# A mixture-of-experts FFN kernel on one core: its second transposes move from TensorE to VectorE squares and a trip through DRAM, the down product two blocks behind

## The chip, the cores and the metric

One core of a Trainium2 chip runs the whole kernel. The metric is the device time in microseconds (us), the median over runs of the program. Besides it there is one profiled execution, whose trace names every instruction, what it waited for, and every transfer.

## The reference

Two layers over x, [4, 512, 256] float32 (2048 tokens). The change touches the second only.

```
x = x + L0_xattn(layernorm(x), ctx_2048, lens)       # rms norms, a 256x256 projection, a decayed scan, a gather
z = layernorm(x)                                      # second layer
probs = softmax(z @ gate_w); top 2 of E = 8 experts, their weights scaled to sum 1
for i in range(8):
    h = silu(z @ w1[i]) * (z @ w3[i])                 # [tokens, 1024]; w1, w3: [256, 1024]
    out = out + (h @ w2[i]) * wi[..., None]           # w2: [1024, 256]; wi is 0 where expert i is not chosen
x = x + out
```

## The kernel before

The first layer, the router and the lists of tokens fill the first 108 us or so. Tokens are sorted by expert into blocks of 128 (at most 39 blocks; 37 here), and a block belongs to one expert. The FFN then runs one step per block, in order. `over_steps` (L288) unrolls step 0 and loops over pairs of steps; a word per step, from a table that VectorE makes, holds the block's expert, the expert of the block before and flags. The order of instructions in each engine's program is fixed by hand, in its own `step` function; semaphores join them.

Products are float32 made of three float32r products (`three`: hi by hi, hi by lo, lo by hi). So each operand exists as a rounded part and a rest: ScalarE copies (`split_hi` for weights, `xT`, `hT`), and VectorE subtracts (`split_lo`, `xT`, `hT`).

What TensorE does in step i, in this order (L1376):

- `up(slot, q, 0)`: half of the gate and up columns for block i, 12 multiplications of 512 columns
- `hT(i-1, 1)`: 4 transposes (with an identity) of the second half of block i-1's hidden rows into PSUM
- `xT(i+1)`: 2 transposes of the next block's input, gathered from DRAM
- `up(slot, q, 1)`: the other half, 12 multiplications
- `hT(i, 0)`: 4 transposes of the first half of block i
- `down(i-1)`: 24 multiplications of 256 columns for the block before, into one PSUM tile

ScalarE in step i: `silu` of half 0, the rounded copy of the transposes of block i-1's half 1, the same for `xT(i+1)`, `silu` of half 1, the copy of block i's half 0, then the weight splits of that step if its flags ask for one, and last `y(i-1)`, which scales the down product. VectorE: `h` (silu times the linear part) of half 0, the rest of `hT(i-1, 1)`, `meta`, the rest of `xT`, `next_index`, `h` of half 1, the rest of `hT(i, 0)`, then `split_lo` where ScalarE split.

The three parts of an expert's weights (w1, w3, w2; 1 MB each) are split into hi and lo during the first three steps of the expert before it, one part a step. SyncE loads them: experts 0 and 1 during the first layer, expert 2 just after step 0's splits, and expert e+3 when expert e+1's last part is split. GpSimd gathers the rows of block i+3 in step i (`block_rows`, L468) and adds the rows of block i-1 to the output in DRAM with an accumulating scatter (`add_rows`, L476). Each scatter waits until the one before has landed. After the last step `drain` does the last half block's transposes and the last down product.

Of the kernel before, what the change touches and what calls it, by code (L numbers as in the profile page):

```python
# [22 lines left out]
P = 128  # L23
B, S, D = 4, 512, 256
# [15 lines left out]
TABLE = 1 + 2 * STEP_PAIRS + 3  # L40

PREV_BIT = 3
F_CHUNK, F_W2, F_W3, F_LOAD, F_RUN = (1 << n for n in range(6, 11))
CHUNK_BIT = 11
OUT_INIT = 32
# [3 lines left out]
RAW_SEM = 48  # L49


def build(nc, x, ctx, lens, w_in, b_in, g_res, g_init, gate_w, w1, w3, w2, out):
# [12 lines left out]
    with stack:  # L65
# [6 lines left out]
        z_dram = nc.dram_tensor("z_rows", (T + P, D), f32, kind="Internal").ap()  # L72
        depool_dram = [nc.dram_tensor(f"depool_rows{b}", (S, D), f32, kind="Internal").ap() for b in range(B)]
# [103 lines left out]
        with ExitStack() as early:  # L177
# [9 lines left out]
        dg = sb("dg", [P, 2, TPB, D], f32)  # L187
# [59 lines left out]
            hT0hi_ready hT0lo_ready hT1hi_ready hT1lo_ready xT_done xThi_ready xTlo_ready  # L247
# [7 lines left out]
        blk_in = [sem(f"blk_in{q}") for q in range(2)]  # L255

# [6 lines left out]
        def raw_load(eng, e, slot, signal, parts=(0, 1, 2)):  # L263

            for m in parts:
                to = raw_dn[:, ds(slot, 1)] if m == 2 else raw_up[:, ds(slot, 1), m]
                eng.dma_start(to, (w1, w3, w2)[m][ds(e, 1)].rearrange("o (k p) n -> p (o k) n", p=P))\
                   .then_inc(signal, 16)

        def step_word(eng, i):  # L270
            entry, top = table[0:1, ds(i, 1)], (3 << CHUNK_BIT) - 1
# [7 lines left out]
        def chunk_of(word):  # L279
            return (word >> CHUNK_BIT).with_bounds(min_val=0, max_val=2)  # L280
# [8 lines left out]
        def over_steps(eng, body):  # L289

            body(0, 0, 0, step_word(eng, 0))
            with eng.Fori(0, STEP_PAIRS) as pair:
                word = step_word(eng, pair * 2 + 1)
                with eng.If(word & F_RUN):
                    body(pair * 2 + 1, 1, pair, word)
                    word = step_word(eng, pair * 2 + 2)
                    with eng.If(word & F_RUN):
                        body(pair * 2 + 2, 0, pair + 1, word)

        def block_count(eng):  # L300
            eng.wait_ge(s["blocks_ready"], 1)
            return eng.value_load(blocks_i[:, :], min_val=E, max_val=BLOCKS)

        def at_end(eng, blocks, drain):

            with eng.If(blocks & 1):
                drain(blocks - 1, 0)
            with eng.If((blocks + 1) & 1):
                drain(blocks - 1, 1)
# [17 lines left out]
        def _(sp):  # L327
# [31 lines left out]
            parts = [(e, m) for e in range(2) for m in range(3)]  # L359
            for k in range(B + 2):  # L360
# [17 lines left out]
                for e, m in parts[max(k - 1, 0):k] if k < B + 1 else parts[k - 1:]:  # L378
# [1039 lines left out]
```

## Time and the profile before

| | |
|---|---|
| median of 3 runs | 485.99 us (485.35 to 486.03) |
| the profiled execution | 486.02 us |
| its span, first to last instruction | 484.3 us |
| mean granted TensorE clock | 0.938 |
| busy: TensorE / VectorE / ScalarE / GpSimd | 87% / 53% / 40% / 32% |

The time outside the span is 1.7 us. In a timeline row the first number is the start in us from the span's start, the second the length, then engine, line, operation, output<-input, shape and count; in brackets stands the idle time of that engine before it and what ended it. PE is TensorE's multiplication, PEld its weight load, DVE VectorE, ACT ScalarE, POOL GpSimd, SPq SyncE's transfers.

### The profile page before, as it was taken

How to read it: one execution, taken by the hardware profiler on the slowest of the kernel's cores; microseconds unless marked ns; L12 is line 12 of the kernel's file. 1: busy time of each engine (PE TensorE's matmuls, PEld its weight loads, DVE VectorE, ACT ScalarE, POOL GpSimd, SP SyncE). 2: the span in 40 equal slices, each digit the busy share in tenths (PEclk: the TensorE clock that was granted, in tenths of full speed). 3: DMA queues.
4: the chain of work that ended last, by engine and by line, in shares of the span. 5: the costliest groups of instructions: out<-in, count | busy, mean ns of one | idle time of the engine just before them, and what ended most of it. 6: DMA issues, size and time to landing. Idle time of an engine off the chain costs nothing.

```text
span 484.3 us, 10407 instructions
## 1 busy us (share of the span) xinstructions
PE 422.8 (87%) x2557; PEld 366.5 (76%) x2558; DVE 257.4 (53%) x673; ACT 192.7 (40%) x334; POOL 157.0 (32%) x130
## 2 busy tenths in 40 slices
PE   0668994339899999999999999999999999999980
PEld 0557874328688988888888888888988888888870
DVE  7877867987753355334553553355355334552230
ACT  3446445212452445324544443454445324542220
POOL 5354540022142234223432432253234223432321
PEclk9979886558999999999999999999999999999996
DMA  6856788400719111811136128113711211111120
GB/s 197 304 175 217 263 260 241 149 23 22 271 26 292 32 22 24 290 32 22 27 103 216 22 46 279 22 22 71 254 22 22 32 32 22 26 29 31 22 32 11
DMA packets 33076, 50.92 MB, mean 105 GB/s; under 512 B 3335, under 2 KB 25095, under 8 KB 33063
## 3 DMA queue, kind: packets, MB, share of 16 engines
q1 hardware_dynamic: 24983, 38.44, 23.7%
q0 software_dynamic: 8080, 12.33, 13.0%
q8 instruction: 5, 0.08, 0.1%
q14 instruction: 8, 0.07, 0.0%
HBM read 39.36 MB, written 11.40 MB: 105 GB/s over the span
## 4 chain that ended last, share of the span: by engine, by line
PE 74%; DVE 5%; issue 3%; DMA 2%; POOL 1%; DVEq 0%; ACT 0%; POOLq 0%; ACTq 0%
PE bank L1322 64%; PE bank L1345 6%; PE bank L1329 2%; PE bank L1255 1%; DMA dg<-depool_rows,plugi 1%; DMA out<-yblk,itok 1%; PE bank L1276 1%; POOL dg L441 1%; DVE split L1117 0%; DVE split L321 0%; DVE batch L985 0%; PE bank L1201 0%; POOL out L480 0%; DVE onehot_lo L981 0%; DVE st L818 0%
## 5 line engine op out<-in xcount | busy, mean ns | idle before, releaser
L1322 PE MATMUL bank<-split,xT_hi 128*128 x592 | 167.0, 404 | 1.5 <-DVE xT_lo L1082 1.4
L1091 DVE TENSOR_TENSOR hmul<-gact,bank 128x512 f32<-128x512 f32 x74 | 50.9, 688 | 145.7 <-ACT gact L609 145.7
L480 POOL DMA_INDIRECT out<-yblk,itok x37 | 78.6, 2123 | 149.7 <-ACT yblk L616 138.0
L1322 PEld LDWEIGHTS bank<-split,xT_hi 128*128 128x128 f32 x592 | 106.9, 190 | 22.9 <-issue 2.3
L1322 PE MATMUL bank<-split,hT 128*128 (+1 forms) x888 | 115.2, 286 | 1.4 <-issue 0.7
L1322 PEld LDWEIGHTS bank<-split,hT 128*128 128x128 f32 x888 | 108.5, 191 | 2.0 <-issue 1.2
L609 ACT ACTIVATE gact<-bank 128x512 f32<-128x512 f32 x74 | 44.2, 598 | 159.4 <-PE bank L1322 159.4
L1322 PE MATMUL bank<-split,xT_lo 128*128 x296 | 94.0, 399 | 0.0
L472 POOL DMA_INDIRECT xblk<-z_rows,gidx x40 | 40.8, 1021 | 107.4 <-DVE gidx L1104 101.5
L321 DVE TENSOR_TENSOR split<-raw,split (+1 forms) x22 | 50.4, 2292 | 37.1 <-ACT split L315 35.9
L1322 PEld LDWEIGHTS bank<-split,xT_lo 128*128 128x128 f32 x296 | 56.1, 190 | 13.6
L1097 DVE TENSOR_TENSOR hT<-bank,hT 128x512 fp32r<-128x512 f32 x74 | 50.6, 684 | 3.7 <-ACT hT L604 3.7
L315 ACT ACTIVATE split<-raw (+1 forms) x24 | 45.9, 1913 | 2.9 <-issue 1.9
L1345 PE MATMUL bank<-ident,hmul 128*128 128x128 f32 x296 | 44.4, 272 | 1.3 <-DVE hmul L1091 1.3
L604 ACT ACTIVATE hT<-bank 128x512 fp32r<-128x512 f32 x74 | 43.9, 593 | 4.1 <-PE bank L1345 3.1
L1345 PEld LDWEIGHTS bank<-ident,hmul 128*128 128x128 f32 x296 | 36.8, 141 | 11.5 <-DVE hmul L1091 1.8
L616 ACT ACTIVATE yblk<-bank,wtok 128x256 f32<-128x256 f32 x37 | 17.6, 476 | 47.4 <-PE bank L1322 35.2
L441 POOL DMA_INDIRECT dg<-depool_rows,plugi x16 | 15.5, 972 | 19.8 <-issue 12.1
L600 ACT ACTIVATE xT_hi<-bank 128x256 fp32r<-128x256 f32 x38 | 14.8, 389 | 15.4 <-PE bank L1329 15.4
L1255 PE MATMUL bank<-gate,batch 128*128 128x8 f32 x64 | 11.2, 312 | 6.8 <-DVE base L875 6.1
L1255 PEld LDWEIGHTS bank<-gate,batch 128*128 128x128 f32 x64 | 10.9, 264 | 7.5 <-DVE base L875 6.4
L1235 PE MATMUL bank<-win,batch 128*128 128x256 f32 x64 | 16.3, 414 | 0.0
(182 smaller groups left out, 311.7 us busy)
## 6 DMA issues: line engine op xcount, KB each, us to landing
raw<-in_L_ffn_w SPq DMA_DIRECT2D x24, 1024.0 KB, 8.1
ctx_sb<-in_ctx SPq DMA_DIRECT2D x4, 1024.0 KB, 6.5
x_all<-in_x SPq DMA_DIRECT2D x4, 512.0 KB, 8.2
depool_rows<-gact SPq DMA_DIRECT2D x4, 512.0 KB, 3.0
out<-x_all SPq DMA_DIRECT2D x4, 512.0 KB, 5.4
z_rows<-z SPq DMA_DIRECT2D x4, 512.0 KB, 3.8
xblk<-z_rows,gidx POOLq DMA_INDIRECT x40, 2.8
out<-yblk,itok POOLq DMA_INDIRECT x37, 4.7
```

Of the source, the lines that this page charges most:

```text
L315: act.activation(split_chunk[:, ds(raw3 * 2 + m, 1)], raw_chunk[:, ds(raw3 + m, 1)], ACT.Copy)\
L321: dve.tensor_tensor(split_chunk[:, ds(raw3 * 2 + m + 3, 1)], raw_chunk[:, ds(raw3 + m, 1)], split_chunk[:, ds(raw3 * 2 + m, 1)].bitcast(f3 ...
L441: pool.indirect_dma_start(dg[:, b % 2, j, :], None, depool_dram[b][:, :], bass.IndirectOffsetOnAxis(ap=plugi[:, n:n + 1], axis=0))\
L472: pool.indirect_dma_start(xblk[:, q, :], None, z_dram[:, :], bass.IndirectOffsetOnAxis(ap=gidx[:, q:q + 1], axis=0))\
L480: pool.indirect_dma_start(out[:, :], bass.IndirectOffsetOnAxis(ap=itok[:, q:q + 1], axis=0), yblk[:, q, :], None, compute_op=ALU.add).then ...
L604: act.activation(hT_hi[:, q, half * KF // 2:(half + 1) * KF // 2], p_hT[half][:, :], ACT.Copy)\
L609: act.activation(gact[:, half * HALF:(half + 1) * HALF], p_gate[half][:, :], ACT.Silu)\
L1091: dve.tensor_tensor(hmul[:, cols], gact[:, cols], p_lin[part][:, :], ALU.mult)\
L1097: dve.tensor_tensor(hT_lo[:, q, ks].rearrange("p k t -> p (k t)"), p_hT[part][:, :], hT_hi[:, q, ks].bitcast(f32).rearrange("p k t -> p (k ...
L1255: mm = pe.matmul(p_logit[:, j * E:(j + 1) * E], zT[:, j, k * P:(k + 1) * P], gate[:, k, :], start=(k == 0), stop=(k == KD - 1))
L1322: mm = pe.matmul(out_, xp, w_, start=start and n == 0, stop=stop and n == 2)
L1345: mm = pe.transpose(p_hT[part][:, k * P:(k + 1) * P], hmul[:, f0:f0 + P], ident[:, :])
```

## The change

1. The hidden rows are no longer transposed by TensorE. After each `h` VectorE transposes the half block in squares of 32 by 32 (`turn`: one instruction over 128x512, out of `hmul` into a new tile `swap_in`). SyncE writes it to DRAM (256 KB) and reads it back into `swap_out` with the squares in their transposed places, in runs of 512 bytes. ScalarE then rounds and VectorE subtracts from `swap_out` in SBUF, where they read PSUM before. The last block alone keeps TensorE's transposes (`hT_last`), with a reordering copy ahead (`perm_last`).
2. The squares of one read-back leave the hidden rows in the order b, j within 128. So w2's rows are loaded in the matching order, as four transfers of 32 partitions each.
3. `down` runs two blocks behind: `down(i-2)` closes step i. `y`, `meta` and `add_rows` follow it. Two steps are unrolled ahead of the loop. On ScalarE `y(i-2)` now stands ahead of the splits of step i.
4. w2 of an expert is split in that expert's own first step (F_OWN), w1 and w3 in the second and third step of the expert before (F_CHUNK, or both together where it has fewer, F_BOTH).
5. SyncE loads expert 0 only. GpSimd loads expert 1 ahead of its part of the lists, and expert e+2 in the first step of expert e, after that step's scatter and after e's w2 is split.

```
         def over_steps(eng, body):
-            body(0, 0, 0, step_word(eng, 0))
+            for i in range(2):
+                body(i, i, 0, step_word(eng, i))
...
+            def exchange(i, q, half):                       # SyncE
+                for part in range(2):
+                    sp.wait_ge(s["swap_ready"], 2 * i + part + 1)
+                    if after(i, 2):
+                        settle(sp)
+                        sp.wait_ge(swapped[q][part], 16 * half)
+                        settle(sp)
+                    sp.dma_start(swap_dram[q, part], swap_in[:, q, part].rearrange("p b k t -> p (b k t)"))\
+                      .then_inc(parked[q][part], 16)
+                for part in range(2):
+                    sp.wait_ge(parked[q][part], 16 * (half + 1))
+                    if after(i, 2):
+                        settle(sp)
+                        sp.wait_ge(s[f"hT{part}lo_ready"], i - 1)
+                    sp.dma_start(swap_out[:, q, part].rearrange("p a k t -> p a (k t)"),
+                                 swap_dram[q, part].rearrange("(a j) (b c) -> (j b) a c", a=NQ, b=NQ))\
+                      .then_inc(swapped[q][part], 16)
...
-            def step(i, q):                                  # GpSimd
+            def step(i, q, half, word):
                 pool.wait_ge(s["xT_done"], i + 2)
                 block_rows(i + 3, 1 - q)
-                if not isinstance(i, int):
-                    add_rows(i - 1, 1 - q)
+                if after(i, 2):
+                    add_rows(i - 2, q)
+                with pool.If(word & F_LOAD):
+                    e = expert(word).with_bounds(min_val=0, max_val=E - 3)
+                    pool.wait_ge(s["lo_ready"], e * 3 + 3)
+                    settle(pool)
+                    pool.wait_ge(s["raw_ready"], RAW_SEM * (e + 1))
+                    settle(pool)
+                    raw_load(pool, e + 2, e & 1, s["raw_ready"])
...
                 silu(i, 0)                                   # ScalarE
-                if later:
-                    hT(i - 1, 1 - q, 1)
                 xT(i + 1, 1 - q)
+                if after(i, 2):
+                    hT(q, half, 1)
                 silu(i, 1)
-                hT(i, q, 0)
+                if after(i, 1):
+                    hT(1 - q, half + q, 0)
+                if after(i, 2):
+                    y(i - 2, q)
+                if not after(i, 1):
+                    act.wait_ge(s["list_mm"], 2)
+                with act.If(word & F_OWN):
+                    split_hi(act, (e & 1) * 3, 2)
                 with act.If(word & F_CHUNK):
                     act.wait_ge(s["raw_ready"], RAW_SEM * (e + 1))
                     split_hi(act, raw3, chunk_of(word))
...
+            def turn(i, q, half, part):                      # VectorE
+                dve.wait_ge(s[f"h{part}_done"], i + 1)
+                if after(i, 2):
+                    dve.wait_ge(parked[q][part], 16 * half)
+                dve.transpose(swap_in[:, q, part].rearrange("p b k t -> p k b t"),
+                              hmul[:, part * HALF:(part + 1) * HALF].rearrange("p (k b t) -> p k b t", b=NQ, t=Q))\
+                   .then_inc(s["swap_ready"], 1)
...
             def step(i, q, half, word):
                 h(i, 0)
-                if later:
-                    hT(i - 1, 1 - q, 1)
-                    meta(i - 1, 1 - q)
+                turn(i, q, half, 0)
                 xT(i + 1, 1 - q)
+                if after(i, 2):
+                    hT(i - 2, q, 1)
                 next_index(i + 3, 1 - q, half + q + 1)
                 h(i, 1)
-                hT(i, q, 0)
+                turn(i, q, half, 1)
+                if after(i, 2):
+                    meta(i - 2, q)
+                if after(i, 1):
+                    hT(i - 1, 1 - q, 0)
+                with dve.If(word & F_OWN):
+                    split_lo(dve, e, (e & 1) * 3, 2)
...
                 up(slot, q, 0)                               # TensorE
-                if later:
-                    hT(i - 1, 1)
                 xT(i + 1, 1 - q, half + q)
                 up(slot, q, 1)
-                hT(i, 0)
-                if later:
-                    down(i - 1, 1 - q, expert_before(word), (word >> PREV_BIT) & 1)
+                if after(i, 2):
+                    down(i - 2, q, expert_before(word), (word >> PREV_BIT) & 1, swapped_lo, (i - 1, i - 1))
...
             def drain(i, q):
-                hT(i, 1)
-                down(i, q, E - 1, (E - 1) & 1, by_halves=True)
+                hT_last(0)
+                hT_last(1)
+                word = step_word(pe, i + 1)
+                down(i - 1, 1 - q, expert_before(word), (word >> PREV_BIT) & 1, swapped_lo, (i, i))
+                down(i, q, E - 1, (E - 1) & 1, (s["drainlo_ready"], s["drainlo_ready"]), (1, 2))
```

`down` now waits for the first half of its transposed rows, runs its first 12 multiplications, and waits for the second half (in the code before only the last block did so). `h` no longer waits for TensorE's transposes. `up` waits for `h` of the block before.

## Rows read from the trace of the kernel before

**Rows 1.** The page's busy times: us, share of the span, instructions.

```profile
PE 422.8 (87%) x2557; PEld 366.5 (76%) x2558; DVE 257.4 (53%) x673; ACT 192.7 (40%) x334; POOL 157.0 (32%) x130
```

**Rows 2.** The page's chain that ended last, by engine.

```profile
PE 74%; DVE 5%; issue 3%; DMA 2%; POOL 1%; DVEq 0%; ACT 0%; POOLq 0%; ACTq 0%
```

**Rows 3.** Timeline of TensorE's weight loads in one step, starts first.

```profile
252.75 2.93 PEld L1322 LDWEIGHTS bank<-split,hT 128*128 128x128 f32 x24
...
255.61 0.77 PEld L1322 LDWEIGHTS bank<-split,xT_hi 128*128 128x128 f32 x4
...
258.30 0.59 PEld L1345 LDWEIGHTS bank<-ident,hmul 128*128 128x128 f32 x4
...
258.86 0.25 PEld L1329 LDWEIGHTS bank<-ident,xblk 128*128 128x128 f32 x2
...
262.31 2.93 PEld L1322 LDWEIGHTS bank<-split,hT 128*128 128x128 f32 x24
```

**Rows 4.** Single lines over the whole run: ns min/median/max, first and last start.

```profile
L315 ACT ACTIVATE split<-raw x21: 1912/1916/1921, 120.0 to 426.0; - x21
...
L616 ACT ACTIVATE yblk<-bank,wtok x37: 474/477/478, 131.5 to 471.2; 128x256 f32<-128x256 f32 x37
...
L426 POOL DMA_DIRECT2D out<-zeros x2: 567/684/801, 16.6 to 17.4; - x2
...
L472 POOL DMA_INDIRECT xblk<-z_rows,gidx x40: 943/994/2127, 103.4 to 462.8; - x40
...
DMA to landing us min/median/max: 2.7/2.8/6.1
```

**Rows 5.** Timeline of a step with a weight split, ScalarE and VectorE.

```profile
262.81 0.69 DVE L1091 TENSOR_TENSOR hmul<-gact,bank 128x512 f32<-128x512 f32 x1 [1.66 <-ACT gact L609]
...
263.35 1.91 ACT L315 ACTIVATE split<-raw  x1
...
265.17 0.77 PEld L1322 LDWEIGHTS bank<-split,xT_hi 128*128 128x128 f32 x4
...
265.64 0.47 ACT L616 ACTIVATE yblk<-bank,wtok 128x256 f32<-128x256 f32 x1 [0.37 <-PE bank L1322]
265.85 2.29 DVE L321 TENSOR_TENSOR split<-raw,split  x1 [1.75 <-ACT split L315]
...
268.29 0.60 ACT L609 ACTIVATE gact<-bank 128x512 f32<-128x512 f32 x1 [2.17 <-PE bank L1322]
...
270.24 0.42 DVE L1082 TENSOR_TENSOR xT_lo<-bank,xT_hi 128x256 fp32r<-128x256 f32 x1
```

**Rows 6.** Windows: us, busy by engine (PE, PEld, DVE, ACT, POOL), clock, DMA share, GB/s.

```profile
120.00:131.30 11.30, 9.50 (x56) 7.71 (x54) 8.42 (x13) 6.37 (x7) 0.94 (x1) 1.00 0.64 239
...
252.00:258.00 6.00, 6.00 (x41) 5.45 (x40) 1.29 (x2) 1.56 (x3) 1.52 (x2) 1.00 1.03 382
...
440.00:449.56 9.56, 9.56 (x60) 8.38 (x59) 3.09 (x8) 2.93 (x6) 2.52 (x3) 1.00 0.17 27
```

**Rows 7.** The page's transfers: KB each, median us from issue to landing.

```profile
depool_rows<-gact SPq DMA_DIRECT2D x4, 512.0 KB, 3.0
```

**Rows 8.** Timeline of GpSimd: the lists' product, and two scatters.

```profile
96.42 1.31 POOL L464 TENSOR_TENSOR batch<-onehot_lo,tiles_b 128x672 bf16<-128x672 bf16 x1 [18.43 <-DVE onehot_lo L981]
...
257.47 1.59 POOL L480 DMA_INDIRECT out<-yblk,itok  x1 [4.08 <-ACT yblk L616]
...
267.06 2.55 POOL L480 DMA_INDIRECT out<-yblk,itok  x1 [4.11 <-ACT yblk L616]
```

**Rows 9.** Timeline of the FFN's start: the input transposes of two steps.

```profile
122.51 0.38 PE L1329 MATMUL bank<-ident,xblk 128*128 128x128 f32 x2
...
134.68 0.38 PE L1329 MATMUL bank<-ident,xblk 128*128 128x128 f32 x2
```

**Rows 10.** Timeline of the last two scatters.

```profile
467.79 1.59 POOL L480 DMA_INDIRECT out<-yblk,itok  x1 [3.98 <-ACT yblk L616]
...
472.67 1.58 POOL L480 DMA_INDIRECT out<-yblk,itok  x1 [3.29 <-issue]
```

More of the change, by code:

```diff
@@ L39 @@
 STEP_PAIRS = BLOCKS // 2
-TABLE = 1 + 2 * STEP_PAIRS + 3
+TABLE = 2 + 2 * STEP_PAIRS + 3
+Q = 32
+NQ = P // Q
 PREV_BIT = 3
-F_CHUNK, F_W2, F_W3, F_LOAD, F_RUN = (1 << n for n in range(6, 11))
+F_OWN, F_CHUNK, F_BOTH, F_LOAD, F_RUN = (1 << n for n in range(6, 11))
 CHUNK_BIT = 11
-OUT_INIT = 32
+OUT_INIT = 48
 CH = -(-S2 // P)
 FULL = S2 // CH
-RAW_SEM = 48
+RAW_SEM = 16 * (2 + NQ)
+KH = KF // 2
 def build(nc, x, ctx, lens, w_in, b_in, g_res, g_init, gate_w, w1, w3, w2, out):
@@ L255, in build @@
         blk_in = [sem(f"blk_in{q}") for q in range(2)]
+        parked = [[sem(f"parked{q}_{part}") for part in range(2)] for q in range(2)]
+        swapped = [[sem(f"swapped{q}_{part}") for part in range(2)] for q in range(2)]
         block = stack.enter_context(nc.Block())
@@ L356, in _ @@
             sp.dma_start(z_dram[T:T + P, :], zeros[:, :]).then_inc(s["z_rows"], 16)
-            parts = [(e, m) for e in range(2) for m in range(3)]
+            parts = [(0, m) for m in range(3)]
             for k in range(B + 2):
@@ L424, in pad_out @@
                 pool.wait_ge(s["pad_ready"], 1)
[L425 to L427 removed]
+                for a, n in ((0, P // 2), (P // 2, P // 4), (P * 3 // 4, P // 4)):
+                    pool.dma_start(out[T + a:T + a + n, :], zeros[0:n, :]).then_inc(s["added_rows"], 16)
             def pow1(b):
@@ L1121, in step @@
             def step(i, q, half, word):
-                later = not isinstance(i, int) or i > 0
-                if not later:
+                if not after(i, 1):
                     dve.wait_ge(s["lo_first"], 2)
@@ L1160, in drain @@
             def drain(i, q):
-                hT(i, q, 1)
+                perm_last(i, 0)
+                perm_last(i, 1)
+                hT(i - 1, 1 - q, 1)
+                hT_last(i, q, 0)
+                hT_last(i, q, 1)
+                meta(i - 1, 1 - q)
                 meta(i, q)
-            blocks = block_count(dve)
+            less_two = blocks_less_two(dve)
             over_steps(dve, step)
-            at_end(dve, blocks, drain)
+            at_end(dve, less_two, drain)
         @block.tensor
@@ L1361, in down @@
                 mm.then_inc(s["y_done"], 1)
+            swapped_lo = s["hT0lo_ready"], s["hT1lo_ready"]
             def step(i, q, half, word):
-                later = not isinstance(i, int) or i > 0
                 slot = word & 1
                 pe.wait_ge(s["xTlo_ready"], i + 1)
-                if later:
+                if after(i, 1):
                     pe.wait_ge(s["lo_ready"], expert(word) * 3 + 2)
+                    pe.wait_ge(s["h0_done"], i)
                 else:
```

226 lines of the change are left out of this document (116 added, 110 removed).

## The prediction

> **What bounds the kernel now.** I read the page's busy times first: TensorE works 87% of the span, VectorE 53%, ScalarE 40%, GpSimd 32% [rows 1]. Then the chain that ended last: TensorE holds 74% of it, no other engine over 5% [rows 2]. Then one step on TensorE's timeline. The down product starts at 252.75 and again at 262.31, so a step takes 9.56 us. Inside it: down 2.86 (to 255.61), half an up product 2.69 (to 258.30), four transposes 0.56 (to 258.86), and 3.45 with two input transposes, the other half of up and four more transposes [rows 3]. The pieces touch each other. There are 37 blocks [rows 4], and 37 x 9.56 = 354 of the 484 us. So in the FFN an instruction that leaves TensorE's stream shortens the step by its own time, unless another engine becomes late.
>
> **What is removed.** Eight transposes in each of 36 steps (the last block keeps its own): 36 x 2 x 0.56 = 40.3 us [rows 3]. The step of TensorE becomes 9.56 - 1.12 = 8.44 us: up 2.69, input transposes about 0.21, up 2.68, down 2.86.
>
> **What takes its place, in a step without a split.** Count from the end of the last down product (0). The first half of up ends at 2.69. The silu starts 3.12 us after down's end, as in the trace (265.17 to 268.29) [rows 5], and ends at 3.72. VectorE's h follows to 4.44 (0.69). The square transpose of 128x512 is not in the trace. Its bounds: below, 0.42, the price of a subtraction of half the size; above, 2.29, the price of four times the elements [rows 5]. I take 0.69, the price of an operation over as many elements; operations without a wait overlap by 0.09. So: square to 5.16, rest of xT to 5.49, rest of the second half of block i-2 to 6.10. TensorE needs that rest when down reaches its second half, at 2.69 + 0.21 + 2.68 + 1.43 = 7.01. No stall, 0.9 us to spare. The new wait of up for h of the block before costs nothing: h of half 0 is done at 4.44, wanted at 8.44.
>
> **In a step behind a split.** This is where I expect part of the gain to be lost. Before, ScalarE split while down ran: the split starts at 263.35, down ends at 265.17 and y comes after [rows 5]. Now y(i-2), which waits for down(i-2), stands ahead of the split. From down's end (265.17): y 0.47 to 0.94, the split some 0.15 later, 1.09 to 3.01 (1.92), then 0.59 until VectorE's split starts (265.26 to 265.85) [rows 5]: 3.60 to 5.89. Behind it in VectorE's order: h 5.80 to 6.49, square 6.52 to 7.21, xT's rest to 7.54, the rest of block i-2's second half 7.45 to 8.14. TensorE wanted it at 7.01: a stall of 1.1 us. The delay does not pile up, as VectorE is done with the step about 0.7 us into the next one. How many such steps: 8 experts split w2 in their own first step, and 7 of them the next expert's w1 and w3 in the next two, 22 in all (before: 21 in the loop [rows 4], one ahead of it). Step 0's falls on a step with no down: 21 x 1.1 = 23 us. The stall could be 0.7 (a split that starts at once, a cheaper square) to 1.6: 15 to 34 us. The clock should stay: in the window from 120 to 131.3 TensorE is idle for 1.8 of 11.3 us and the granted clock is 1.00 [rows 6].
>
> Weighed against this: the Trainium skill (VectorE: DVE Perf Modes, The three transpose paths) says that VectorE transposes squares of 32 only, 128x128 in bf16 in 311 ns, and in its rules to use TensorE for 128x128. By its figure, four times 311 ns, the square would be an estimated 1.24 us, the stall 1.6 us and the sum about 480. No row shows which is right.
>
> **The trip through DRAM.** A store of 512 KB from SyncE lands in 3.0 us [rows 7], a gather of 128 KB in 2.8 (median) to 6.1 beside a load [rows 4]. So about 3 us each for 256 KB out and back, 6 beside a load. The read of half 0 is issued once half 1's store is, about 0.5 us into the next step; ScalarE wants it at 6.6, 6 us later. The read of half 1 starts about 4, lands at 7 to 10 and is wanted at 4.1 of the step after, 12.6: hidden, with 2.5 us to spare in a load. Traffic: 1 MB a step beside the 27 GB/s at 17% share of a plain step [rows 6] is another 124 GB/s of the 382 that a load reaches; not a bound. If landing took over 9 us, TensorE would wait in every step. Behind SyncE's wait for a landed store stand only its own next transfers (the weight loads are gone from its queue); behind ScalarE's wait for a read stand silu of half 1 or y(i-2).
>
> **GpSimd's loads.** The load waits for VectorE's w2 split, and behind it on GpSimd stand the next gather and the next scatter. A load is now six transfers. One of 64 rows takes GpSimd 0.57 to 0.80 us [rows 4]; these have 256 pieces. Bounds: 0.7 each (flat), 2.7 (by the row). I take 1.0, a gather's price for 128 rows [rows 4], thus 6 us. It starts behind VectorE's w2 split, about 6, so the next gather is issued at about 12 and, behind 3 MB in its queue at 382 GB/s [rows 6] shared with the exchanges, lands about 20. It is wanted at 9.5 + 9.5 + 2.7 = 21.7: hidden. Expert 1's load lies in the 18.4 us in which GpSimd waits ahead of the lists (end at 96.42) [rows 8]: hidden even at 2.7 each. Scatters: issued one block later, same prices.
>
> The Trainium skill (DMA: Bandwidth & Descriptors, SWDGE vs HWDGE vs iDMA) says that GpSimd writes its descriptors into SBUF, from which VectorE can lock it out, while SyncE's transfers never touch that path; this speaks against moving the loads. The trace agrees in kind: a scatter's issue takes 1.59 us alone and 2.55 beside VectorE's split [rows 8].
>
> **Start and end.** From xT of step 1 to that of step 2 the trace has 12.17 us (122.51 to 134.68) [rows 9], 2.6 more than a step: transposes waited for h behind a split. That wait goes; step 0's w2 split now holds VectorE until about 123.7 and up(2) waits for xT's rest some 1.2 us. Net -1.4. In the drain, the reordering copy (0.7) and the single PSUM tile between two downs (0.65) replace two waits of 1.5 together: 0. The last two scatters are 4.88 us apart [rows 10] since one waits for the other's landing (3.9); two y's now come 3.5 apart after the last product, so the last scatter starts about 2.9 after TensorE's end and not 1.7: +1.2.
>
> **Sum.** 484.3 - 40.3 - 1.4 + 1.2 + 23 = 466.8 of span; 1.7 outside it as before (486.0 against 484.3): 468.5. The profiled run is 486.02, the median 485.99: no correction.
>
> **Rivals.**
> - All hidden: the split stall does not come about, since ScalarE or VectorE gets there earlier than my chain says (an earlier y, a square of 0.42 and overlaps). For it: 0.9 us of slack in plain steps. Against: the order of y and split. 468.5 - 23 = 445.5.
> - GpSimd late: 2.7 us a transfer. The gather is issued at 22.4 and lands at 25.2, 3.5 after it is wanted; the split stall in that step vanishes: 2.5 x 6 loads = 15, so 483.5. For it: 1.59 against 2.55, a row price by row. Against: gathers of 128 rows take no longer than 64 rows by more than 0.3.
> - A dear square: each 0.1 us beyond 0.69 costs 2.1 us over the 21 steps, and beyond 1.56 the plain steps stall too. It decides at about 1.52 us: 468.5 + 21 x 0.83 = 486. At the upper bound, 2.29: 21 x 1.6 + 14 x 0.73 = 44 more, 512, slower than before. For it: no row shows the operation. Against: every row of VectorE goes by elements.
> - A slow trip: over 9 us a landing in each step, also slower, about 500. Against: 3.0 for twice the bytes.
>
> **Chances.** Forecast 0.48 (461 to 477); all hidden 0.16; GpSimd late 0.12; dear square 0.20, of which 0.09 stays below 486; slow trip 0.04. The range 446 to 484 takes in the forecast, half of all hidden, most of GpSimd late and the cheap part of the dear square: 0.78. A change under 0.2% (1 us) can't be told from none: 0.02; faster 0.83, slower 0.15.
>
> **What would show it.** Right: 8.44 us between downs in plain steps and about 9.5 behind each split, with TensorE idle in the middle of down, released by VectorE's rest of hT; squares at 0.7; six issues of about 1 us on GpSimd; transfers landing in 3 us; clock 1.00 throughout. Wrong: TensorE idle ahead of the input transposes (gather late), ahead of down's first half (trip), or in plain steps (square); or a clock below 1.00 in the FFN.

## The result and the profile after

The changed kernel takes 508.16 us (median of 4 runs, 506.67 to 508.52) against 485.78 for the kernel before (4 runs). The ratio is 1.046, interval 1.0445 to 1.0475: slower. The forecast was 468.5, with 446 to 484 as its range. The profiled execution has a span of 506.6 us (508.28 in all), 39.8 more than the 466.8 of the sum. One run of the first experiment (501.62 us) was in a slower state of the chip and is left out of its median; with it that median is 497.36, the 497.4 that two later expectations name.

The page's busy times of the changed kernel, to be laid beside [rows 1], and its chain by engine, beside [rows 2]:

```profile
PE 408.6 (81%) x2269; PEld 345.9 (68%) x2270; DVE 307.4 (61%) x750; ACT 194.3 (38%) x334; POOL 167.1 (33%) x173
...
PE 39%; DMA 19%; DVE 14%; issue 11%; ACT 7%; DVEq 4%; POOL 3%; ACTq 1%; SPq 0%; POOLq 0%
```

TensorE has 288 instructions fewer and is busy 14 us less, yet the span grew by 22. Its part of the chain fell from 74% to 39%. Transfers took 19%, VectorE 14% and issue 11%. The kernel no longer has one bound: TensorE now waits for others. For what, its waits in the FFN say (us in total, times, longest):

```profile
PE bank L1400 <- DVE hT L1155: 14.7, 16, 4.6
PE bank L1400 <- issue: 12.6, 17, 1.1
PE bank L1400 <- DVE split L340: 6.3, 1, 6.3
```

**The plain step.** The timeline of TensorE's matmuls from one down product to the next:

```profile
211.19 1.19 PE L1400 MATMUL bank<-split,xT_hi 128*128 x4
...
214.08 0.38 PE L1407 MATMUL bank<-ident,xblk 128*128 128x128 f32 x2
...
217.09 3.02 PE L1400 MATMUL bank<-split,hT 128*128 x24
219.96 1.09 PE L1400 MATMUL bank<-split,xT_hi 128*128 x4
```

219.96 - 211.19 = 8.77 us without a gap: up 2.89, input transposes 0.13, up 2.88, down 2.87. The forecast was 8.44. Eight transposes were worth 9.56 - 8.77 = 0.79, not 1.12. The same view of the kernel before shows what the two groups of four took in the step of [rows 3]:

```profile
258.53 0.60 PE L1345 MATMUL bank<-ident,hmul 128*128 128x128 f32 x4
258.96 0.38 PE L1329 MATMUL bank<-ident,xblk 128*128 128x128 f32 x2
...
261.98 0.60 PE L1345 MATMUL bank<-ident,hmul 128*128 128x128 f32 x4
262.34 3.11 PE L1322 MATMUL bank<-split,hT 128*128 x24
```

From start to start that is 0.43 and 0.36.

**The new operations.** Two of the page's groups (busy us, mean ns of one, idle before), and two of its transfers (KB each, median us to landing):

```profile
L643 ACT ACTIVATE hT<-swap_out 128x512 fp32r<-128x512 f32 x72 | 45.3, 629 | 28.8 <-DMA swap_out<-swap_rows 26.3
L1147 DVE STREAM_TRANSPOSE swap_in<-hmul 128x512 f32<-128x512 f32 x74 | 52.7, 712 | 4.4
...
swap_rows<-swap_in SPq DMA_DIRECT2D x74, 256.0 KB, 2.0
swap_out<-swap_rows SPq DMA_DIRECT2D x74, 256.0 KB, 3.2
```

The square takes 0.71 us where 0.69 was taken, and out and back take 2.0 and 3.2 us where 3 was taken for each. Both medians are as good as the forecast. But ScalarE waited 26.3 us for reads that came late: the median hides them.

**Behind a split.** The timeline of such a step, three engines:

```profile
228.99 0.48 ACT L662 ACTIVATE yblk<-bank,wtok 128x256 f32<-128x256 f32 x1 [1.89 <-PE bank L1400]
229.49 1.92 ACT L334 ACTIVATE split<-raw  x1
...
231.89 2.29 DVE L340 TENSOR_TENSOR split<-raw,split  x1 [3.14 <-ACT split L334]
...
235.87 0.67 DVE L1155 TENSOR_TENSOR hT<-swap_out,hT 128x512 fp32r<-128x512 f32 x1
...
236.68 1.70 PE L1400 MATMUL bank<-split,hT 128*128 x12 [0.46 <-DVE hT L1155]
...
238.95 1.19 PE L1400 MATMUL bank<-split,xT_hi 128*128 x4 [0.57 <-issue]
```

Down begins its second half at 236.68, when VectorE's rest of hT is there. That is the stall that the forecast described, by the chain that it described: y, split, VectorE's split, h, square, rests. Only 0.46 us of it shows as a wait. The second half of down then takes 238.95 - 0.57 - 236.68 = 1.70 instead of 1.43, and ahead of the next up product TensorE stands 0.57 us for nothing that the profile shows ("issue"). It has this idle time in 17 steps and in no plain one. In two of them (from 328.61 and from 369.06) the half comes so little late that no wait is listed, and 0.55 and 0.53 us of idle stand there all the same.

What "issue" hides can be read from TensorE's sequencer (PEldq), by the source views of three lines: the branch of the loop over pairs of steps (L307), the read of the next step's word (L287, at 248.2 in the first case and 210.0 in the second) and that step's first semaphore wait (L1445). The numbers are the length in ns and the start in us. First ahead of the step that starts at 249.65 (down's second half has 1.70 us from 246.82 on, then 1.12 us of "issue"):

```profile
L307 PEldq COMPARE_BRANCH  x1: 213/213/213, 247.8 to 247.8; - x1
...
L1445 PEldq EVENT_SEMAPHORE  x1: 51/51/51, 249.3 to 249.3; - x1
```

Then ahead of the plain step that starts at 211.19:

```profile
L307 PEldq COMPARE_BRANCH  x1: 213/213/213, 209.6 to 209.6; - x1
...
L1445 PEldq EVENT_SEMAPHORE  x1: 51/51/51, 210.9 to 210.9; - x1
```

In the plain step the sequencer does this work of over 1 us while down still runs. Behind the wait in down's middle it begins 0.7 us ahead of down's end, and what is left of it then leaves TensorE idle: 0.94 to 1.12 us ahead of the 8 steps at which the loop turns, 0.53 to 0.58 ahead of the other 9, which have no L307.

**The expert of three blocks.** The same view around the switch to the last expert:

```profile
436.96 0.47 ACT L662 ACTIVATE yblk<-bank,wtok 128x256 f32<-128x256 f32 x1 [2.13 <-PE bank L1400]
...
438.02 1.91 ACT L334 ACTIVATE split<-raw  x1 [0.58 <-issue]
...
440.50 2.29 DVE L340 TENSOR_TENSOR split<-raw,split  x1 [3.48 <-ACT split L334]
...
443.03 2.07 PE L1400 MATMUL bank<-split,xT_hi 128*128 x4 [6.27 <-DVE split L340]
```

Here the split of w3 falls in the expert's last step, and the very next instruction of TensorE needs it. TensorE waits 6.27 us. The first matmuls behind the wait take 2.07 us for four against 1.19. The window behind it has a granted clock of 0.50, the lower level, 1.2 GHz (columns as in [rows 6]):

```profile
443.00:446.00 3.00, 2.97 (x7) 2.40 (x8) 0.00 (x0) 0.00 (x0) 0.00 (x0) 0.50 0.00 0
```

Half an up product takes 5.26 us there (443.03 to 448.29) instead of 2.9. From input transposes to input transposes the step takes 17.8 us.

**The first load.** The timeline of GpSimd's issues, SyncE's read back and TensorE:

```profile
126.73 2.36 POOL L282 DMA_DIRECT2D raw<-in_L_ffn_w  x4
...
128.30 7.48 SPq L418 DMA_DIRECT2D swap_out<-swap_rows  x2
...
140.12 0.44 PE L1407 MATMUL bank<-ident,xblk 128*128 128x128 f32 x2 [1.69 <-DMA xblk<-z_rows,gidx]
...
149.41 2.92 PE L1400 MATMUL bank<-split,hT 128*128 x12 [4.62 <-DVE hT L1155]
```

And the landing times of all 74 read backs, from the view of their line:

```profile
DMA to landing us min/median/max: 2.6/3.2/12.4
```

The read issued at 128.30, behind the 3 MB of the load, is the one that took 12.4 us. The gather comes late, then half of hT; two steps take 10.8 and 16.1 us. Behind the wait of 4.62 the clock falls here too:

```profile
149.40:152.15 2.75, 2.74 (x12) 2.64 (x13) 1.94 (x5) 0.00 (x0) 0.99 (x1) 0.50 0.41 116
```

The second half of down takes 2.74 us and the next half of up 4.05, together 2.5 more than at full clock.

**Granted clock and drain.** A long window of the changed kernel:

```profile
200.00:400.00 200.00, 182.89 (x1015) 155.10 (x1016) 117.02 (x218) 82.55 (x133) 68.47 (x65) 1.00 0.65 196
```

In the 200 us from 200 to 400 TensorE stood for 17 us in small pieces and the clock was 1.00, as in all of the time from 156 to 443. Between 118 and 484 us it fell behind the two long waits alone. The timeline of VectorE and TensorE ahead of the last transposes:

```profile
484.73 1.18 DVE L1163 COPY gact<-hmul 128x512 f32<-128x512 f32 x2 [2.55 <-issue]
...
485.40 1.67 PE L1423 MATMUL bank<-ident,gact 128*128 128x128 f32 x8 [3.14 <-DVE gact L1163]
```

VectorE stands 2.55 us between its last step and the reordering copy, and nothing that the profile shows releases it.

### The profile page after: what moved, and what is told of

The parts are those of the page before. It is cut to its first block, busy times and chain, and to the rows that moved or that the text cites. A ratio compares the mean times of both kernels' runs of the same rounds, so it can differ in the third digit from the quotient of the medians.

```text
span 506.6 us, 10801 instructions
## 1 busy us (share of the span) xinstructions
PE 408.6 (81%) x2269; PEld 345.9 (68%) x2270; DVE 307.4 (61%) x750; ACT 194.3 (38%) x334; POOL 167.1 (33%) x173
## 4 chain that ended last, share of the span: by engine, by line
PE 39%; DMA 19%; DVE 14%; issue 11%; ACT 7%; DVEq 4%; POOL 3%; ACTq 1%; SPq 0%; POOLq 0%
PE bank L1400 33%; DMA swap_out<-swap_rows 11%; ACT split L334 6%; DMA swap_rows<-swap_in 6%; PE bank L1333 2%; DVE hmul L1139 2%; DVEq L288 2%; POOL dg L473 2%; PE bank L1293 1%; DVEq L340 1%; DVE swap_in L1147 1%; DVE hT L1155 1%; DVE onehot_lo L793 1%; ACTq L334 1%; DMA out<-yblk,itok 1%
## 5 line engine op out<-in xcount | busy, mean ns | idle before, releaser
L1400 PE MATMUL bank<-split,xT_hi 128*128 x592 | 172.6, 414 | 21.9 <-issue 12.6
L1400 PE MATMUL bank<-split,hT 128*128 (+1 forms) x888 | 119.2, 288 | 15.8 <-DVE hT L1155 14.7
L1400 PEld LDWEIGHTS bank<-split,hT 128*128 128x128 f32 x888 | 114.3, 193 | 23.3 <-issue 19.2
L340 DVE TENSOR_TENSOR split<-raw,split x22 | 50.5, 2294 | 63.2 <-ACT split L334 63.2
L513 POOL DMA_INDIRECT out<-yblk,itok x37 | 59.1, 1598 | 86.1 <-ACT yblk L662 79.6
L1155 DVE TENSOR_TENSOR hT<-swap_out,hT 128x512 fp32r<-128x512 f32 x72 | 48.8, 677 | 17.0 <-ACT hT L643 17.0
L643 ACT ACTIVATE hT<-swap_out 128x512 fp32r<-128x512 f32 x72 | 45.3, 629 | 28.8 <-DMA swap_out<-swap_rows 26.3
L1147 DVE STREAM_TRANSPOSE swap_in<-hmul 128x512 f32<-128x512 f32 x74 | 52.7, 712 | 4.4
L276 POOL DMA_DIRECT2D raw<-in_L_ffn_w x14 | 10.9, 779 | 22.8 <-issue 22.8
L1407 PE MATMUL bank<-ident,xblk 128*128 128x128 f32 x76 | 14.8, 277 | 2.8 <-DMA xblk<-z_rows,gidx 2.8
L1333 PEld LDWEIGHTS bank<-gate,batch 128*128 128x128 f32 x64 | 12.3, 296 | 6.6 <-DVE base L925 5.7
```

The source lines that it names most:

```text
L340: dve.tensor_tensor(split_chunk[:, ds(raw3 * 2 + m + 3, 1)], raw_chunk[:, ds(raw3 + m, 1)], split_chunk[:, ds(raw3 * 2 + m, 1)].bitcast(f3 ...
L513: pool.indirect_dma_start(out[:, :], bass.IndirectOffsetOnAxis(ap=itok[:, q:q + 1], axis=0), yblk[:, q, :], None, compute_op=ALU.add).then ...
L643: act.activation(hT_hi[:, q, ks].rearrange("p k (a t) -> p a k t", a=NQ), swap_out[:, q, part], ACT.Copy)\
L1147: dve.transpose(swap_in[:, q, part].rearrange("p b k t -> p k b t"), hmul[:, part * HALF:(part + 1) * HALF].rearrange("p (k b t) -> p k b ...
L1155: dve.tensor_tensor(hT_lo[:, q, ks].rearrange("p k (a t) -> p a k t", a=NQ), swap_out[:, q, part], hT_hi[:, q, ks].bitcast(f32).rearrange( ...
L1333: mm = pe.matmul(p_logit[:, j * E:(j + 1) * E], zT[:, j, k * P:(k + 1) * P], gate[:, k, :], start=(k == 0), stop=(k == KD - 1))
```

## The experiments

Twelve kernels ran, in three groups of four; each group had its own runs of the kernel before (485.94, 484.92 and 485.61 us). Where a kernel ran once, no interval is given.

### Order of y, and the splits

**y behind the splits** (the changed kernel with this one part undone):

```
 def step(i, q, half, word):               # ScalarE
...
-    if after(i, 2): y(i - 2, q)
     (w2's split, next expert's split)
+    if after(i, 2): y(i - 2, q)
```

> The changed kernel with one edit on ScalarE: y(i-2) stands behind the splits of step i again, as in the kernel before, all else kept. Theory A (the order of y and split costs the time): the splits fall under down, the 17 steps of 10 to 12 us behind a split return to 8.8, 30 us less, and about 3 more at the last expert: 475 (470 to 482). Theory B (VectorE is full: squares, two rests and a split don't fit into 8.8 us, wherever the split starts): 500 or more. Theory C (the trips through DRAM are late; the chain that ended last gives transfers 19%): no more than 5 us change.

Measured: 496.07 us (493.18 to 498.64, three runs), ratio 1.021 [1.014, 1.027]. So 12.1 us came back, not 33, and none of the three theories has the number. Most steps behind a split are back at 8.7 to 8.8 us. TensorE's waits show what came up in their place (besides, the wait for the w3 split is down from 6.27 us to 3.24):

```profile
PE bank L1400 <- DVE hT L1155: 15.7, 6, 2.7
```

The timeline around the second load shows what it hangs on:

```profile
174.84 2.81 POOL L282 DMA_DIRECT2D raw<-in_L_ffn_w  x4
...
181.43 2.74 SPq L418 DMA_DIRECT2D swap_out<-swap_rows  x2
...
188.86 0.63 ACT L643 ACTIVATE hT<-swap_out 128x512 fp32r<-128x512 f32 x1 [4.19 <-DMA swap_out<-swap_rows]
...
192.30 2.29 DVE L340 TENSOR_TENSOR split<-raw,split  x1 [2.09 <-ACT split L334]
...
197.09 1.68 PE L1400 MATMUL bank<-split,hT 128*128 x12 [2.68 <-DVE hT L1155]
```

The landing times of the two read backs from 180 to 186:

```profile
DMA to landing us min/median/max: 5.6/5.6/5.6
```

There were 16 short waits; now there are 6 long ones, one for each load. The store issued at 174.78 beside a load let the read back start only at 181.43, 6.6 us later (a plain step: 2.8), the read took 5.6 (plain: 3.0), and ScalarE waited 4.19 us for the half. Behind that stand the step's split on ScalarE and then on VectorE (192.30), and behind those the other half's rest, for which TensorE waited 2.68.

**y behind the splits, and w1 and w3 of the next expert in this expert's first and second step** (so the three-block expert has both ahead of its last step, and each first step has two splits):

```
-dve.tensor_scalar(f_m, j_, 2.0, None, ALU.is_equal)
+dve.tensor_scalar(f_m, j_, 1.0, None, ALU.is_equal)
...
(f_both: j = 0 and last; some_: j >= 0 or last; f_chunk: j <= 1)
```

> The kernel above, and the next expert's w1 is split in the expert's first step and w3 in its second (before: second and third), w2 of the expert itself still in the first. If the 6.3 us wait at the last expert comes from w3 being split in the third and last step of a three-block expert: 5 to 7 us less than the kernel above, about 469, with no step over 10 us behind block 5. If two splits in one step bring the stall back: 7 experts x 1.5 = 10 more, so 475 to 480. If that wait is for w2: no change.

Measured: 480.57 us, ratio 0.988 [0.985, 0.991], 1.2% less than the kernel before: small, but clear of the noise. The wait for the w3 split is gone, and from 145 us to 450 the granted clock is 1.00. The start has two splits in one step and takes 12.3 us for it (3.81 of them idle, and a clock of 0.66 from 125 to 135 us).

The number lies beside the 475 to 480 of two splits in one step, but by luck: that was counted from 475, and the kernel above had taken 496. What was not foreseen is that the late reads would cost so little. They are as late as before (timeline of ScalarE and TensorE behind the second load):

```profile
188.67 0.63 ACT L643 ACTIVATE hT<-swap_out 128x512 fp32r<-128x512 f32 x1 [4.99 <-DMA swap_out<-swap_rows]
...
193.72 1.69 PE L1400 MATMUL bank<-split,hT 128*128 x12 [0.45 <-DVE hT L1155]
```

ScalarE waits 30.7 us for reads in 11 waits, against 28.2 in 6 above. But the late read comes two steps behind the load, and in this kernel that step has no split. So no split stands behind the late half, TensorE waits 0.45 us and not 2.68, and the step takes 10.1 us and not 12.5. In the kernel above a split follows each of the six late reads by about 1 us. The long waits therefore need two things in one step: a half that comes late, and a split behind it.

**The kernel before, with y ahead of its splits:**

```
 hT(i, q, 0)                               # ScalarE, step, kernel before
+if later: y(i - 1, 1 - q)
 with act.If(word & F_CHUNK):
...
(a wait for y_done ahead of w2's split goes too)
-if later: y(i - 1, 1 - q)
```

> The kernel before with y (which waits for the end of the down product) ahead of ScalarE's split instead of behind it. Theory that the order costs by itself, whatever else was changed: the splits start some 2.9 us later in 21 steps, VectorE's rest and the transposes of the next half behind them, +10 to +25 us (496 to 511). Rival, that the order only costs because down runs two blocks behind and takes VectorE's rest in its middle: within 3 us of 486.

Measured: 510.62 us, ratio 1.052 [1.050, 1.054]. The order alone costs 25.7 us in a kernel without square, trip or GpSimd's loads, 1.28 us for each of the 20 splits that a y stands ahead of (the first of the 21 has none). TensorE's waits:

```profile
PE bank L1320 <- issue: 11.6, 29, 0.6
PE bank L1343 <- DVE hmul L1089: 1.9, 4, 1.4
```

Little of the wait for VectorE is left in the records. What they show is 29 times some 0.4 us of "issue", behind transposes that start as soon as h is there (h ends at 240.17, they start at 240.22). A stall of this kind is seen in the step's length and not in a wait.

**The changed kernel with y behind the splits, and the splits spread as in the kernel before** (w1, w3, w2 of the next expert in the first, second and third step; expert 0's one step later, its own w2 in its first). This and the kernels that build on it are written for experts of three blocks or more, as these inputs have.

```
+zero_ = (e_ == 0); k_ = j_ - zero_
-f_own: j_ == 0
+f_own: j_ == 0 and zero_
-f_m: j_ == 2          f_chunk: j_ <= 2 and low2 and (j_ >= 1 or last_)
+f_m: min(max(k_, 0), 2)   f_chunk: k_ <= 2 and low2 and (k_ >= 0 or last_)
```

> The changed kernel with two parts undone: y(i-2) is behind the splits again, and the splits are spread as before (w1, w3, w2 of the next expert in this expert's first, second and third step, one in each; expert 0's one step later, since its own w2 is split in its first). Against the run with the splits in the first two steps (480.6), which has the double split of an expert's first step left: 8 x (1.1 + 0.5) of stall and lost lead go, and 3.3 us of the start (12.1 us for the second step): 464 to 467. Rival, that a load beside the exchange, not the double split, makes these stalls: 476 to 481.

Measured: 492.41 us, ratio 1.016 [1.014, 1.018]: a miss by 25 us, the rival's way and beyond its 476 to 481. The six long waits are all there (15.5 us for VectorE's hT, 6 times), and behind three of them half an up product takes 3.3 to 4.1 us instead of 2.9. So the double splits were not what held TensorE. Behind each of the late reads stands a split again, here that of w2.

### The loads beside the trip

**The changed kernel, loads of experts 2 to 7 cut to an eighth of each row:**

```
-raw_load(pool, e + 2, e & 1, s["raw_ready"])
+raw_load(pool, e + 2, e & 1, s["raw_ready"], f1=F // 8, d1=D // 8)   # columns 0:f1, 0:d1
```

> The changed kernel; the loads of experts 2 to 7 move an eighth of each row (the rest of the weights stays stale, so the output is not the reference's), with the same six transfers and as many pieces. If traffic beside the exchanges costs (a read back takes 8 to 12 us beside a load, 3 else): the two steps after the first load lose 9 us less and the ones two steps behind a load 1 to 2 less each, 508 - 14 = 494. If GpSimd's six issues cost (late gathers): no change, 508.

**The changed kernel without the exchange** (SyncE moves nothing; the readers take `swap_in`):

```
-exchange(i, q, half)                      # SyncE
...                                        # and VectorE's square waits for no store
-act.activation(hT_hi[...], swap_out[:, q, part], ACT.Copy)
+act.activation(hT_hi[...], swap_in[:, q, part], ACT.Copy)
```

> The changed kernel without the trip: SyncE moves nothing in the FFN, ScalarE and VectorE read the squares in SBUF where the transpose put them (so squares stay in untransposed places and the output is not the reference's). If the trip is late only beside loads: 9 us less at the start and 5 at later loads, 494, and the steps behind a split stay at 10.2 to 10.7. If it is late in most steps: every step at 8.8, under 480.

Measured, one run each: 496.32 and 497.08 us against 485.94. With y ahead, either half of the collision taken away gives 12 and 11 us, and the stalls behind splits and the 6.3 us ahead of the last expert stay.

**y behind the splits, loads cut to an eighth**, and **y behind the splits, no exchange** (both edits as above):

> The changed kernel with y behind the splits (497.4) and with the loads of experts 2 to 7 cut to an eighth of each row (most of the weights of those experts stay stale). If the 2.7 to 3.9 us stall per expert two steps behind a load comes from the read back of half of h beside the load's traffic: 6 x 3.3 and most of the start's 4.5 us go, 475 and no step over 12 us but that behind the three-block expert. If it comes from VectorE's two splits in a row: 490 to 497.

> The changed kernel with y behind the splits (497.4), without the exchange: ScalarE and VectorE read the squares as VectorE wrote them (h's squares are not swapped, so down works on a wrong order). The loads stay whole. If it is the trip that the loads hurt, all stalls but that behind the three-block expert go, as with the loads cut to an eighth (461.1): 459 to 464. If the loads also hurt something else (the gather, TensorE's own stream), it stays above 475.

Measured, one run each: 461.09 and 466.46 us. The first is 14 us below the 475 expected of it, the second 2.5 above its range. Both have the same waits left. Those of the first:

```profile
PE bank L1400 <- DVE split L340: 3.2, 1, 3.2
PE bank L1423 <- DVE gact L1163: 3.2, 1, 3.2
```

And the landing times of its 74 read backs:

```profile
DMA to landing us min/median/max: 2.7/3.0/3.9
```

The six long waits are gone with the bytes although all 36 issues on GpSimd are still there, and gone without the trip although all the bytes are. So, with a split in the step, it is the meeting of the two: 496.1 - 461.1 = 35 us. (The second of the two runs has half an up product of 5.28 us for 2.9 behind the three-block expert, at a clock of 0.50, which is somewhat under half of what sets them apart.)

**Splits spread as before, y behind them, and the load cut in three:** 1 MB (w1, then w3, then w2) in each of three steps, instead of 3 MB in one.

```
 with pool.If(word & F_LOAD):              # now in three steps of an expert
...
+    piece = chunk_of(word)
+    for m, flag in enumerate(((piece + 3) & 2, piece & 1, piece & 2)):
+        with pool.If(flag):
+            pool.wait_ge(s["raw_ready"], RAW_SEM * (e + 1) + 16 * m)
+            settle(pool)
+            raw_load(pool, e + 2, e & 1, s["raw_ready"], (m,))
```

> The kernel with y behind the splits and the splits spread over an expert's first three steps (492.4), and with GpSimd's load of the expert after next cut in three of 1 MB, one in each of those steps (w1, w3, w2), instead of 3 MB in one step. Theory: 3 MB in front of the exchange's transfers hold them up past the point where the down product wants the half; 1 MB holds them up for a third as long, which the slack of a plain step covers. Then all seven stalls of 3 to 4 us, the slow clock behind them and the first load's 8 us go: 455 to 462, faster than the kernel before. Rival, that any transfer of 4 KB pieces beside the exchange delays it by several us: the stalls come three times per expert, 485 to 500.

Measured: 464.73 us (463.05 to 466.59), ratio 0.956 [0.954, 0.957]: 4.4% faster than the kernel before, and 27.7 us less than the same kernel with whole loads. TensorE's waits from 140 to 440 (besides, one of 0.2 for VectorE's rest of hT):

```profile
PE bank L1407 <- issue: 3.8, 7, 1.4
```

ScalarE still waits for reads (13.1 us in 11 waits), but the slack takes most of it. It is 2.7 us over the upper end of what was expected. From the input transposes of the fourth block to the last, 304.2 us are left for 34 steps (298.2 at 8.77). Two of them are 1.6 us too long each. One has a short wait in down's middle and 0.94 of "issue" behind it. The other has no wait, but 1.37 of "issue": there TensorE's read of the step's word took 1.02 us, where its median is 0.30 (from 200 to 400 us in the changed kernel). What held that read is open.

```profile
L287 PEldq TENSOR_LOAD <-table x1: 1023/1023/1023, 359.0 to 359.0; - x1
```

**The same, with y(i-2) ahead of the splits** (the order of the changed kernel):

> The run with spread loads, with y(i-2) ahead of the splits again as in the changed kernel. It prices the order of y and split with the load's interference and the three-block expert out of the way. By the steps of the changed kernel's trace (10.2 to 10.7 against 8.77 behind a single split, 22 splits): 22 x 1.65 = 36 us more than the run with spread loads. By the forecast's stall of 1.1: 24 us more. Rival, that the order costs little once the trip is on time: under 8 us.

Measured: 493.80 us (492.54 to 494.83), ratio 1.017 [1.015, 1.019], 29.1 us more. The waits of TensorE from 140 to 460:

```profile
PE bank L1407 <- issue: 14.3, 20, 1.0
PE bank L1407 <- DVE hT L1162: 10.0, 13, 1.2
```

With the loads out of the way, the order costs 29.1 us over the 20 splits with a y ahead, 1.45 each: between the 24 and the 36 expected, and far from the rival's 8. More of it is "issue" than is a wait for VectorE.

### The price of a transpose, and the drain

**The kernel before with two of eight transposes:**

```
 def hT(i, part):                          # TensorE, kernel before
-    for k in range(KF // 2):
+    for k in range(KF // 2 if isinstance(i, int) else 1):
```

> The kernel before, with one of the four transposes of each half of h left out of three (two of eight stay; the rest of h is not transposed, so the down product works on stale parts). Nothing else changes: no trip, no square, no other order. It measures what a transpose in the stream is worth. If its price is that of the weight loads, as forecast (0.14 us each), six fewer in 36 steps give 30 us: 455.5. If it is that of the starts of TensorE's segments in the two traces (0.79 us for eight), they give 0.79 x 3/4 x 36 = 21 us: 464.5.

Measured: 466.24 us (465.9 to 466.96), ratio 0.962 [0.960, 0.963], 18.7 less than its 484.92. That is 2.3 short of the price by the starts of matmuls (21 expected), and far from the 30 by the starts of weight loads.

**The run with spread loads, with 18 loop passes for 19:**

```
-with eng.Fori(0, STEP_PAIRS) as pair:
+with eng.Fori(0, STEP_PAIRS - 1) as pair:
```

> The run with spread loads, with the loop over pairs of steps cut from 19 passes to 18, which the 37 blocks of these inputs need (the last pass finds nothing to do on any engine). Theory, that VectorE's 2.55 us of idle ahead of the reordering copy are partly the empty pass (a word read, a branch): 0.8 to 1.3 us less than the run with spread loads. Rival, that it is the jump into the drain's own code: within 0.3 us.

Measured: 463.23 us (461.94 to 466.81), ratio 0.954 [0.952, 0.957] against 0.956 [0.954, 0.957]; the intervals overlap, so the time does not tell. The place does: on the timeline VectorE's idle ahead of the reordering copy fell from 2.56 to 1.30:

```profile
443.46 1.20 DVE L1170 COPY gact<-hmul 128x512 f32<-128x512 f32 x2 [1.30 <-issue]
```

So a pass that finds nothing to do costs about 1.3 us, and here it lies on the path. What the other 1.3 are (the end of the loop, the branches ahead of the drain) was not tried.

## Why the prediction was wrong

The span came out 39.8 us above the sum. By its own steps:

1. **"8 transposes x 36 steps at 0.56 per four": mis-sized, +11.2.** I read 0.56 from the starts of TensorE's weight loads [rows 3]. They run ahead of the matmuls, in that step by 0.03 us for down, 0.23 for the transposes and 0.10 for the input transposes. So a difference of their starts is not the time of the work between. By matmul starts in the same trace the two groups are 0.43 and 0.36, 0.79 together. The run with two of eight transposes bears this out. 34 steps x 0.33 = 11.2.
2. **"21 steps behind a split x 1.1": the right mechanism, too small, +7.2.** The place, the chain and the engine that is waited for are as described. 17 steps (without those in points 3 and 4) exceed 8.77 by 30.2 us together, 1.8 each. The wait at down's middle is 0.35 to 1.76 in 15 of them and too short to be listed in two (forecast 1.1). What I left out is what comes behind it: a second half of down of 1.70 instead of 1.43, and 0.53 to 1.12 of "issue" ahead of the next up. The sequencer's rows show what that is: the step's own branches and the read of its word, which down covers in a plain step and no longer covers behind a wait. The count was off by one as well: step 1 has no y either, so 20 splits stand behind one. Freed of the rest, the order costs 29.1 us (the last pair of experiments) and by itself, in the kernel before, 25.7.
3. **"and 7 of them the next expert's w1 and w3 in the next two": not all alike, +9.0.** In an expert of three blocks w3 falls in the last step, and TensorE's next instruction needs it. I counted the splits and did not ask of each when it is wanted. y ahead is half of it (the wait is 6.27 with it and 3.24 without), the new place of the split the other half: with w3 in the second step the wait is gone. Of the 9.0, the wait is 6.3 and the fallen clock 2.4.
4. **"3 MB in its queue ... shared with the exchanges, lands about 20 ... hidden": failed, +9.3 in the trace of the changed kernel.** I added the exchange's traffic as a rate (124 GB/s of 382) and gave each transfer of the trip up to 6 us beside a load. A read of 256 KB behind a load took up to 12.4, its store ahead of it up to 4.7. Of the 9.3, two waits are 1.7 and 4.6 and the fallen clock 2.5. The collision is dearer than the 9.3 shows: with y behind the splits, the same collision costs 35 us in one comparison (496.1 against 461.1) and 27.7 in another. With y ahead the steps are longer, and ScalarE's waits for five of the six late reads (3.3 to 3.9 us) reach TensorE as 1.8 at most. The two faults cover each other, and this is why undoing either alone gave only 12 us (496.1 and 496.3) and both 47.
5. **Start and drain: -1.8 and +4.6.** The start is 5.4 us shorter up to the input transposes of the fourth block (129.30 against 134.68 [rows 9]) where the sum had 3.6, as the first down product has moved one step on. From the last input transposes to the end it is 30.4 us against 24.6, where I had +1.2: one more down product (2.9) stands there, and TensorE stands 3.14 ahead of its last transposes, of which I had foreseen 0.7. The empty loop pass was in both kernels; in the kernel before VectorE stands 3.67 us there for ScalarE's copy, which covers it.

-1.8 + 11.2 + 7.2 + 9.0 + 9.3 + 4.6 = 39.5 of 39.8.

"The clock should stay" failed too, in points 3 and 4, for 4.9 us together. The row behind it had TensorE idle for 1.8 of 11.3 us in small pieces, and small pieces did leave the clock at 1.00 here. The waits of 4.62 and 6.27 us, which the forecast did not have, did not.

**What held.** The square at 0.71 (0.69), so the rival of a dear square is out. The Trainium skill (VectorE: DVE Perf Modes, The three transpose paths) gives 311 ns for 128x128 in bf16, by which I had estimated 1.24 us for the square of 128x512; here a stream transpose of 128x512 in f32 took 0.71, so the measurement decides. GpSimd's six issues take 0.58 to 0.80 us each (1.0): the rival of a late GpSimd is out, and though the gather of the first load came 1.69 us late, it did so by landing. Plain steps have no stall, and the trip in them is hidden. The rival "all hidden" is what the kernel becomes once y stands behind the splits and the loads are out of the trip's way: 461.1, where I had 445.5; 16 us too low, 11 of which are the price of the transposes.

**The side that decided it.** None of the rivals was the right one. The prediction said what would show it wrong ("TensorE idle ahead of down's first half (trip)"), but its rival of a slow trip asked for 9 us in every step. A trip that is slow only beside a load wants another sum: with y behind the splits it is six steps of 12.5 to 14.6 us in place of 8.8. The chance of a result slower than before, 0.15, was too low because the late split, the late read and the late half share the same slack of 0.9 us in down's middle, and I had asked of each by itself whether it fits.

## What to carry to other kernels

Price an instruction that leaves TensorE's stream by the starts of matmuls on either side of it, not by those of weight loads. When a small transfer with a due time shares the DMA engines with bulk loads, take its landing time beside a load from the trace, and if there is none, cut the loads so that one piece is shorter than the slack: here three pieces of 1 MB instead of one of 3 MB were worth 27.7 us. Or keep other work of the same engines out of the step in which a transfer can be late. On an in-order engine, put what waits for a late event (y, which needs the end of down) behind what is ready (the split), and ask of each moved piece of work not how long it is, but in which step it is wanted; when two such faults are in a kernel, undo both before judging either.

## What was not expected of the hardware

- A wait in TensorE's stream costs more than the wait: 0.4 to 1.8 us at the middle of down, then 0.27 more for the 12 multiplications behind it and 0.53 to 1.12 of "issue" ahead of the next product, in which the sequencer does branches and a read that it otherwise does ahead of time. In the changed kernel this "issue" is 12.6 us in 17 places, in the kernel before with y ahead 11.6 in 29.
- A DMA of 256 KB that takes 3.0 us alone takes 5.6 to 12.4 beside a load of 3 MB in pieces of up to 4 KB, and 3.9 at most beside the same number of transfers with an eighth of the bytes. So it is not the number of issues. The pieces shrank with the bytes, and no run tells these two apart.
- Waits of 4.6 and 6.3 us were followed by a granted clock of 0.50. Of the seven waits of 2.6 to 3.2 in the kernel with y behind the splits, four were followed by a clock of 0.50 to 0.80 and three by 1.00. After a wait of 3.2 in one kernel without the collision it stayed at 1.00, and after one of 3.3 in the other it was 0.50. The many up to 1.8 left the clock at 1.00.
- A loop pass in which there is nothing to do takes about 1.3 us on VectorE.
